# First step of a state-space mixer: slot 4 ahead of the softplus, weight splits moved between engines, one load moved in its queue

## The reference

```python
proj = x @ W_in.T                                # 256 -> 512 val, 512 gate, 32*128 B, 32*128 C, 32 dt
val, gate, Bp, Cp, dt = split(proj)
val = silu(causal_conv4(val) + conv_b)           # 32 heads of 16
dt  = softplus(dt + dt_bias)
ld  = dt * -exp(A_log)
# per head: Y = ((C B^T) * exp(cum_l - cum_m), m <= l) val + D val
Y = Y * silu(gate);  out = Y @ W_out.T
x = layernorm(x + out)
x = layernorm(x + attention(x, ctx_512, ctx_512))
x = layernorm(x + moe(x))                        # 8 experts, top 2, and a shared expert
```

## Time and profile before

| | |
|---|---|
| three runs | 742.12, 743.87, 744.98 us; median 743.87 |
| the profiled execution | 742.52 us, of which the profiled span is 740.7 |
| TensorE, matmuls | 97% of the span |
| VectorE, ScalarE, GpSimd | 78%, 60%, 51% |
| granted TensorE clock, mean | 0.999 |
| TensorE's waits, 0 to 70 us | 7.0 us together, 2.8 of them at the start |
| TensorE's waits, 60 to 400 us | none |

### The profile page before, as it was taken

The page is one execution under the profiler, slowest core; times in us unless marked ns, Lnnn a source line. Parts: engine busy times, 40 slices in busy tenths (PEclk is TensorE's granted clock), DMA queues, the critical chain, the costliest instruction groups (busy, mean ns, idle before and its releaser), DMA issues. The chain is left out here.

```text
span 740.7 us, 17060 instructions
## 1 busy us (share of the span) xinstructions
PE 717.5 (97%) x5874; PEld 396.3 (54%) x5874; DVE 574.1 (78%) x1104; ACT 442.1 (60%) x870; POOL 379.2 (51%) x420
## 2 busy tenths in 40 slices
PE   8899999999999999999999999999989999999897
PEld 3455555555656555565656555565553333335464
DVE  5677768686776868677676868879888999897877
ACT  7834546754444575454458455455458777778686
POOL 2868427483342748333364965555430331377754
PEclk9999999999999999999999999999999999999999
DMA  6695331214642122353212323533004300000001
GB/s 207 187 225 173 85 58 57 57 57 91 174 89 57 57 57 57 88 168 98 52 61 57 87 85 56 108 67 74 1 3 143 104 24 24 23 1 2 29 31 57
DMA packets 34298, 57.91 MB, mean 78 GB/s; under 512 B 7056, under 2 KB 11920, under 8 KB 33680
## 3 DMA queue, kind: packets, MB, share of 16 engines
q1 hardware_dynamic: 33680, 57.08, 30.3%
q10 hardware_dynamic: 576, 0.31, 0.1%
HBM read 54.10 MB, written 2.36 MB: 76 GB/s over the span
## 5 line engine op out<-in xcount | busy, mean ns | idle before, releaser
L303 POOL TENSOR_TENSOR cum_rows<-cum_rows,cum_t 128x512 f32<-128x512 f32 x128 | 136.3, 1075 | 195.3 <-DMA cum_rows<-cum_scratch 195.3
L833 PE MATMUL pring<-xt_hi,w_hi 128*128 (+1 forms) x576 | 171.7, 380 | 0.0
L833 PE MATMUL pring<-xt_lo,w_hi 128*128 (+1 forms) x576 | 171.4, 379 | 0.0
L833 PE MATMUL pring<-xt_hi,w_lo 128*128 (+1 forms) x576 | 171.4, 379 | 0.0
L675 DVE TENSOR_TENSOR bt<-pring,bt 128x512 f16<-128x512 f32 x128 | 88.0, 687 | 69.8 <-ACT bt L460 69.6
L460 ACT CAST bt<-pring 128x512 f16<-128x512 f32 x128 | 74.5, 582 | 112.9 <-PE pring L833 112.5
L679 DVE TENSOR_TENSOR ct<-pring,ct 128x512 f16<-128x512 f32 x128 | 88.1, 688 | 52.6 <-ACT ct L464 52.3
L875 PEld LDWEIGHTS pscore<-ct,bt 128*128 128x128 f16 x1536 | 95.8, 98 | 34.7 <-issue 6.4
L875 PE MATMUL pscore<-ct,bt 128*128 128x128 f16 x1536 | 106.7, 219 | 3.4 <-issue 2.1
L464 ACT CAST ct<-pring 128x512 f16<-128x512 f32 x128 | 74.7, 584 | 52.9 <-PE pring L833 52.9
L833 PEld LDWEIGHTS pring<-xt_lo,w_hi 128*128 128x128 f16 x576 | 56.3, 98 | 68.0
(11 more groups left out here) (172 smaller groups left out, 961.7 us busy)
## 6 DMA issues: line engine op xcount, KB each, us to landing
cum_rows<-cum_scratch SPq DMA_DIRECT2D x32, 1024.0 KB, 8.0
w_raw<-in_w_in SPq DMA_DIRECT2D x35, 256.0 KB, 6.5
q_rows<-in_xt SPq DMA_DIRECT2D x4, 512.0 KB, 11.0
acc<-in_x SPq DMA_DIRECT2D x1, 2048.0 KB, 8.4
vals<-in_vals SPq DMA_DIRECT2D x16, 128.0 KB, 2.1
out<-acc SPq DMA_DIRECT2D x7, 256.0 KB, 2.2
w_raw_e<-in_w_up SPq DMA_DIRECT2D x1, 1024.0 KB, 6.9
w_raw_e<-in_w_gate SPq DMA_DIRECT2D x1, 1024.0 KB, 5.0
```

The source lines that it names most:

```text
L303: nc.gpsimd.tensor_tensor(rows[:, par, :, q], rows[:, par, :, q], own, ALU.subtract).then_inc(sem("since"), 1)
L833: mm = nc.tensor.matmul(bank[name][:], w[:, c, k, cols], x[:, k, bass.ds(n % TB, 1), :].rearrange("p o n -> p (o n)"), start=(i == 0), sto ...
```

## The change

TensorE runs two warm-up matmuls instead of three. In its first step it projects slot 4 directly behind the step widths of block 2, in front of score group 2, the turn of val and the step widths of block 3. At the end of the step it waits for `xt_lo`, since x of block 1 is now split by ScalarE and VectorE.

ScalarE treats chunks 2 to 5 in one pass; takes slot 4 and decay 3 in front of the softplus of blocks 1 to 3; splits x of block 1 in the place of W_out's cast, which moves to the end of the step.

VectorE forms the low parts of chunks 2 (in front of the convolution), 3, 4 and 5; it takes slot 4 and weighing 3 in front of step sizes, rates and sums, has slot 5's low parts between the sums, and subtracts for x of block 1.

GpSimd no longer forms low parts 2 to 5; it does 6 in exponents(0, 0), 7 between the two calls, 8 in exponents(0, 1). It does not split x of block 1, and W_out's low part moves behind exponents(1, 0).

SyncE issues the load of x behind that of rows (1, 0). The loop over the groups is opened for its first round, with the same contents.

```diff
 # SyncE
-            sp.dma_start(acc[:], io["x"]).then_inc(sem("in_x"), 16)
-            sp.dma_start(expo[:], io["expo"]).then_inc(sem("in_x"), 16)
             sp.wait_ge(sem("cum_out"), 32)
...
+            next_rows(1, 0)
+            sp.dma_start(acc[:], io["x"]).then_inc(sem("in_x"), 16)
+            sp.dma_start(expo[:], io["expo"]).then_inc(sem("in_x"), 16)
+            next_rows(1, 1)
+            refill_chunks(0)
 # GpSimd
-                pool.wait_ge(sem("xt_late"), 2 * t - 1)
+                pool.wait_ge(sem("xt_late"), 2 * t - 3)
...
-            pool.wait_ge(sem("w_ready"), 2)
-            for c in range(2, 6):
-                lo_part(0, c)
             pool.wait_ge(sem("cum_t"), 1)
+            pool.wait_ge(sem("w_ready"), 6)
             exponents(0, 0, {3: 6})
-            exponents(0, 1, {1: 7, 3: 8})
-            split_x(1)
+            lo_part(0, 7)
+            exponents(0, 1, {1: 8})
+            pool.wait_ge(sem("cum_t"), 2)
+            exponents(1, 0)
             pool.wait_ge(sem("wo_hi"), 1)
             nc.gpsimd.tensor_tensor(wo_parts[:, 1], wo, wo_parts[:, 0], ALU.subtract).then_inc(sem("wo_lo"), 1)
-            pool.wait_ge(sem("cum_t"), 2)
-            exponents(1, 0)
             exponents(1, 1)
 # ScalarE
-                if first and c < 2:
+                if first and c < 6:
...
-                act.wait_ge(sem("dt_mm"), TB)
-                softplus(slice(L, TOK), 3)
                 evac_b(0, 4)
                 evac_c(0, 4)
                 decays(0, 3)
+                act.wait_ge(sem("dt_mm"), TB)
+                softplus(slice(L, TOK), 3)
                 evac_b(0, 5)
                 evac_c(0, 5)
                 decays(0, 4)
-                act.wait_ge(sem("in_wo"), 32)
-                nc.scalar.copy(wo_parts[:, 0], wo).then_inc(sem("wo_hi"), 1)
+                split_x(1)
                 evac_b(0, 6)
+                evac_c(0, 6)
                 decays(0, 5)
-                evac_c(0, 6)
                 decays(0, 6)
                 evac_b(0, 7)
                 evac_c(0, 7)
                 decays(0, 7)
+                act.wait_ge(sem("in_wo"), 32)
+                nc.scalar.copy(wo_parts[:, 0], wo).then_inc(sem("wo_hi"), 1)
 # VectorE
+                first_low(2)
                 for k in range(4):
                     convolve(0, k)
                 gate_silu(0)
+                first_low(3)
                 low_b(0, 0)
                 low_c(0, 0)
                 sums_turned(0, 1)
+                first_low(4)
                 val_silu(0)
-                for s in (1, 2, 3):
+                low_b(0, 1)
+                low_c(0, 1)
+                first_low(5)
+                for s in (2, 3):
                     low_b(0, s)
                     low_c(0, s)
                 weigh(0, 0)
                 weigh(0, 1)
                 pad_values(0)
                 weigh(0, 2)
+                low_b(0, 4)
+                low_c(0, 4)
+                weigh(0, 3)
                 step_sizes(slice(L, TOK), 3)
                 rates(slice(L, TOK), 3)
                 sums(1)
-                low_b(0, 4)
+                low_b(0, 5)
                 sums(2)
-                low_c(0, 4)
+                low_c(0, 5)
                 sums(3)
-                weigh(0, 3)
-                low_b(0, 5)
-                low_c(0, 5)
                 weigh(0, 4)
                 low_b(0, 6)
                 low_c(0, 6)
+                split_x(1)
 # TensorE
             warm(1)
-            warm(2)
...
                 step_widths(1)
                 step_widths(2)
+                pair(0, 4)
                 scores(0, 2)
                 turn_values(0)
                 step_widths(3)
                 for s in range(4, SLOTS):
-                    pair(0, s)
+                    if s > 4:
+                        pair(0, s)
...
-                pe.wait_ge(sem("xt_late"), 2)
+                pe.wait_ge(sem("xt_lo"), 2)
...
-            pe.wait_ge(sem("xt_late"), 6)
+            pe.wait_ge(sem("xt_late"), 4)
```

More of the change, by code:

```diff
@@ L243, in load_keys, with refill_chunks @@
                         sp.dma_start(k_rows[r:r + 8, 8 * half:8 * half + 8, :, kv, :].rearrange("d b t n -> d (b t) n"), src).then_inc(sem("k_load"), 16)
-            with sp.Fori(0, GROUPS - 1) as g:
-                next_rows(g * TB + 1, 0)
-                next_rows(g * TB + 1, 1)
+            def refill_chunks(g):
                 for c in range(CHUNKS):
@@ L252, in _ @@
                                  io["w_in"][bass.ds(g + 1, 1), :, c].rearrange("g p k n -> (g p) (k n)")).then_inc(chunk_loaded(c), 16)
+            next_rows(1, 0)
[3 more added lines that the diff above has]
+            refill_chunks(0)
+            with sp.Fori(2, TB + 1) as t:
+                next_rows(t, 0)
+                next_rows(t, 1)
+            with sp.Fori(1, GROUPS - 1) as g:
+                next_rows(g * TB + 1, 0)
+                next_rows(g * TB + 1, 1)
+                refill_chunks(g)
                 with sp.Fori(2, TB + 1) as t:
```

## The result

| | before | after |
|---|---|---|
| median of 8 executions | 743.02 us (741.68 to 745.69) | 747.25 us (745.85 to 747.38) |
| the profiled execution, its span | 742.52, 740.7 | 747.26, 745.5 |
| mean granted TensorE clock of it | 0.999 | 0.995 |

The ratio is 1.006, with an interval of 1.0044 to 1.0075: the change makes the kernel 0.6% slower, 0.65 us beyond the top of the range. The forecast was 744.2: +0.4 us on a median of three runs, 743.87. Against the median of eight, 743.02, the change cost 4.2.

What follows compares the result with a forecast made beforehand. TensorE, busy 97%, was taken to bound the kernel. Out_project of step 1 at 60.0 instead of 59.32 gave +0.7, lowered to +0.4 for more room below; against the median 743.87 the forecast was 744.2 us, range 741.0 to 746.6.

Steps and rivals of the forecast that it cites:

- Val of step 1: TensorE's first work of step 1: to start at 42.5 instead of 45.08, 2.6 us early.
- the wait for the convolution: TensorE before slot 1 in the first step: a wait of over 1 us for VectorE's convolution, until 14.7.
- the sum at the gate: Out_project of step 1, waiting for W_out's low part: start at 60.0 instead of 59.32, a loss of 0.7 us.
- last sum ends: VectorE's running sums in step 0: the last ends at 38.7 instead of 36.42, with 37.0 as the other end.
- store, to the rows' issue: Storing the sums before the row load: 2.3 us with x no longer behind it, ends 1.6 and 3.3.
- row load: Load of rows (1, 0) with x right behind: 9.4 us, landing at 50.4; 7.8 with the queue empty.
- low part of W_out: GpSimd's operation behind exponents(1, 0): 2.13 us, ending at 59.9, with TensorE 0.1 later.
- Rival 2: Load of rows (1, 0) shares the engines with x and takes 11.4: gate at 62.0, +2.7, 746.6; chance 0.15.
- The worst sum: Out_project's gate with every term at its unfavourable end: opens at 60.9, a loss of 1.6 us.
- Rival 1: Out_project's gate open in time (sums unhindered, fast store, 7.8 for the rows): gain 2.4, 741.5; chance 0.25.
- Rival 3: TensorE's clock stays at 1.2 GHz through the first four projections: about +3.5, 747.4; chance 0.03.
- Rival 4: Gate never closes and step 1's two short waits go too: gain 3.0, perhaps 4, 740; chance 0.07.

Runs made afterwards that it cites:

- e1: The changed kernel with only W_out's low part moved back in front of exponents(1, 0) on GpSimd; 742.71 us, ratio 0.9996 against the kernel before.
- e7: The kernel before with only W_out's low part put behind exponents(1, 0) on GpSimd; 744.35 us, ratio 1.0024.
- e3: The changed kernel with the edits of e1 and e2 together (W_out's low part in front, x loaded early); 741.54 us, ratio 0.9977 against the kernel before.
- e6: e3 with the third warm-up matmul back; 741.79 us, ratio 0.9988 against the kernel before.
- e5: e4 with 8 more useless matmuls in front of out_project of step 1; 745.65 us, ratio 1.0039 against the kernel before.
- e10: e3 with VectorE's small dskip scaling moved ahead of the split of x of block 1; 741.32 us, ratio 0.9983 against the kernel before.
- e4: The changed kernel with 12 useless matmuls filling TensorE's wait at score group 1 of step 1; 744.93 us, ratio 1.0039 against the kernel before.
- e8: The kernel before with only the load of x moved behind rows (1, 0), SyncE's loop opened for its first round; 742.02 us, ratio 0.9997.
- e2: The changed kernel with the load of x right behind that of W_out, W_out's low part left late; 744.56 us, ratio 1.0026 against the kernel before.
- e12: The kernel before with x loaded behind W_out and the dskip scaling early, nothing of the change; 742.93 us, ratio 1.0017.
- e9: e3 with slot 4 back behind the softplus on TensorE, ScalarE and VectorE; 744.06 us, ratio 1.0019 against the kernel before.
- e11: e9 with the dskip scaling moved ahead of the split of x of block 1; 742.67 us, ratio 0.9992 against the kernel before.

## Why the prediction was wrong

**Right.** The place and the mechanism: TensorE stands at out_project of step 1 for W_out's low part, which stands on GpSimd behind rows that come late (e1 takes the whole loss away, e7 makes 1.8 us of it in the kernel before). Val of step 1 at 43.25 (said 42.5), one warm-up less worth nothing (e3 against e6), the waits for x of block 2 and for the weighing covered by slot 4, the sums later than before, exponents(1, 0) at 7.3 (52.56 to 59.88), and no new stall in steps 2 and 3. Slot 1 started at 14.79, said 14.7, but in this execution by luck: the wait for the convolution that was given as a sign did not occur. The records turned short only at 11.23, so TensorE was busy until 14.79, and the convolution had ended at 14.48 (12.18 + 2.30). In e1 to e5 and e10, with the same instructions up to there, it waited 0.26 to 1.35 us for it.

**The step that failed is the sum at the gate**, "60.0 − 59.32 = +0.7", which measured +3.16:

| term | said | measured | |
|---|---|---|---|
| last sum ends | 38.7 | 39.60 | +0.9 |
| store, to the rows' issue | 2.3 | 2.1 | −0.2 |
| row load | 9.4 | 10.8 | +1.4 |
| exponents(1, 0) | 7.3 | 7.3 | 0 |
| low part of W_out | 2.13 | 2.56 | +0.4 |
| TensorE starts | 60.0 | 62.48 | +2.5 |

The table is of one execution. In four profiles with the same lists up to the rows (the changed kernel, e1, e4, e5) the last sum ended between 38.20 and 39.60, so the 38.7 is inside what this kernel does. Out_project behind the shut gate started at 62.48, 61.59 and 60.61 (the changed kernel, e4, e5). What was short in each of them is the row load and the low part.

*The row load* is the largest. 9.4 was the row with three blocks of x behind it; with 2 MB behind, it took 10.3 to 10.8 from the issue to GpSimd's start in five kernels (the changed one, e1, e4, e5, e8), and 8.5 to 8.9 where x was loaded early (e2, e3, e6, e10; 9.2 in e12). The Trainium skill (DMA: Bandwidth & Descriptors, "Queues, rings and completion order") says that descriptors are consumed in ring order; that x behind the rows then costs them nothing was the prediction's inference from it. These runs put about 2 us on it, so the measurement decides against that inference. Rival 2 had the mechanism and was given 0.15. That it almost had the landing too (52.4; it was 52.56) is luck: it had 11.4 for a load that took 10.8, and the sums were 0.9 late.

*The sums* took 1.15, 1.22 and 0.79 us where they had taken 0.73, 0.73 and 0.62, though GpSimd was busy beside them in both kernels. What differs is where in GpSimd's instruction a sum starts. The three end 0.27, 0.28 and 0.28 us after the end of the instruction that GpSimd was running when they started (36.30, 38.02 and 39.32), and so do the three of the kernel before. So a sum's length is what GpSimd's instruction has left, and a shift of the start by 2 us gave other remainders; taking over the old length was the error. Score group 5 stands behind them on VectorE, so its wait, said to be 0.2, was 1.38, and val of step 1 came 0.75 later than said. *The low part* took 2.55 or 2.56 in the changed kernel, e4, e5 and e7, where GpSimd took it up while VectorE was at its subtraction for y (59.34 to 60.44 in the changed kernel), and 2.12 at the same late place in e2, where that subtraction was over (56.13 against 57.19). *The store* was shorter, but not for the reason given: with no x behind it, it took 3.0 in e8 and in e9, and 2.1 in e11, which has e9's lists up to there. What sets its time stays open.

**What was left out is the clock.** The prediction had a rival for the clock at the start and none for a fall later, though it forecast a wait of "some 3 us". It also took that wait to be one, at out_project. It is two, since ScalarE's first decay stands ahead of slot 1's casts: 2.93 and then 1.53, with 1.44 us of work between. At 1.2 GHz out_project and the matmuls behind it cost 1.56 us more, in this execution; the mean clock is 0.994 or 0.995 in all eight. That this is a cost of its own is read from its rows directly. That the fall belongs to the waits is shown in part: with the first one filled (e4, e5) no mean clock is below 0.997, and the span is 1.85 to 2.35 us less by the median, though the gate is shut; with the low part in front (e1) all ten executions are at 0.999 or 1.000. Against it stands that the kernel before lost the clock in 34 of 112 executions without these waits.

The +0.7 and the table's 2.5 make the gate's 3.2, and with 1.56 for the clock the whole 4.7. The forecast had gone from +0.7 to +0.4 because "there is more room below my terms than above them". That was the wrong way to lean: the ends below (7.8 for the load, 37.0 for the sums) stood for links with nothing beside them, and the load, the sums and the low part all had something beside them. The worst sum, 60.9, was passed by 1.6 us.

**Rivals.** Rival 1 (the gate open in time, 741.5) could not come true by the rows alone: e2 had them 3.2 us earlier than the changed kernel and TensorE still waited 3.13. And its price was too good: with the low part in front (e1) out_project began at 58.83, not 56.9, because of the decay on ScalarE; only with x early and the scaling moved (e10) was it at 56.33. Rival 3 happened in part: in the profiled execution the records turn short at 11.23, later than the 8.6 of before, but slot 1 started only 0.3 us behind the end of the convolution, so it cost next to nothing. Rival 4 is refuted for the change as it stands; its neighbour e3 is 0.2% under the kernel before.

**What stays open.** Whether out_project is really 0.9 us early in e8: profiles of kernels with the same first step differ by more than that (60.61 to 62.48 above), and its median shows nothing. And by what the clock falls in nine executions of e2 and not in the tenth, and in about three of ten executions of the kernel before.

## What to carry to other kernels

An instruction moved behind a wait inherits everything that the wait hangs on, so price the whole chain with what will lie beside each link, and lean to the contended row: here the row load and the low part had a new neighbour, and the sums met their old one at another moment. A stall of some 3 us on TensorE can have a second price in the clock that it comes back with, half of the first one here; look at the granted clock behind every wait that a change adds, and in all executions of the kernel before as well. And before an operation goes behind such a chain, look for the empty stretch in front of it: GpSimd had 13 us of nothing from 39 us on, and using them gave back the whole 0.6%.

## What the runs showed of the hardware

- The clock fell in the wait of 2.93 us in the changed kernel (at 58.8, 2.2 us into it), after one of 2.12 us in e4 with TensorE already at work again, after one of 1.33 us in e10 likewise (at about 551.8), and not in one of 3.13 us in e2 or of 1.85 in e1. In the changed kernel it was at the lower level for 6.8 us (58.8 to 65.7, worked out from the slices).
- At the start, the first matmuls of val and gate with short records come at 11.23 us in the profiled execution of the changed kernel, 9.58 in e1, 8.89 in e5 and 8.34 in e4, with the same instructions ahead of them. The granted clock of the slices is 1.00 throughout there, so this is read from the records' lengths alone.
- The scaling of 128 x 4 took 0.15 us alone and 0.88 to 1.86 beside GpSimd (e1, e3, e6, e9, e12), and ended each time within 0.03 us of GpSimd's instruction (e12: 44.12 and 44.11, e3: 47.32 and 47.30, e9: 49.43 and 49.41). The Trainium skill (SBUF — State Buffer, "SBUF: two separate sides") says that the shared port pair is an exclusive lock and that "whichever … starts first gets the pair for the whole instruction"; these rows agree to the end of the instruction.
- The running sums of blocks 1 to 3, 42 of them in the 14 profiles, took 0.62 to 1.33 us and ended 0.27 to 0.29 after the GpSimd instruction that was running when they started. The sum of block 0 in the changed kernel, with GpSimd idle, took 0.42.
- A row load of 1 MB took 8.5 to 9.2 us from its issue to GpSimd's start with an empty queue (e2, e3, e6, e10, e12), and 10.3 to 10.8 with 2 MB issued 0.4 us behind it in the same queue (the changed kernel, e1, e4, e5, e8).
